# An attention layer whose query maxima and head results no longer pass TensorE's transposes

## The chip, the cores and the metric

The kernel runs on one core of a Trainium2 chip. The metric is the device time of one execution in microseconds (us); the median of several runs is given. The core has TensorE (matrix products), VectorE, ScalarE and POOL (elementwise work), and SyncE (SP), which here only issues DMA transfers.

## The reference

```python
x = L0_attn_hidden_states                          # (4, 2048, 256), fp32
xn = _layernorm(x, axis=-1)
qkv = (xn @ W_qkv).reshape(B, S, 3, NUM_HEADS, HEAD_DIM)   # 16 heads of 16
scores = jnp.einsum('bhqd,bhkd->bhqk', q, k) + compute_bias(rel_emb, S, S)
attn = jax.nn.softmax(scores, axis=-1)
out = jnp.einsum('bhqk,bhkd->bhqd', attn, v)       # -> (4, 2048, 256)
attention = out @ W_out
router_probs = softmax(xn @ router_w)              # top 2 of 8, normalised; their sum scales the FFN
ffn = (gelu(xn @ w1 + b1) @ w2 + b2) * sum(combine)
return x + attention + ffn
```

The bias depends on key position minus query position through 32 buckets; beyond 128 positions it is constant on each side. There are 4 x 16 = 64 pairs of batch and head, called heads here, each of 2048 queries and 2048 keys.

## The kernel before

It has three parts, each a block of its own.

**Part one** normalises x, makes q, k and v, and computes x + ffn into `base_rows` in DRAM. q and k are kept in DRAM (`qk_parts`) transposed, each fp32 split into a high and a low part, since TensorE multiplies the type `fp32r`; three pairs of parts stacked over 16 dimensions make the 48 rows (`ROWS`) of a product. v stays in SBUF (`v_all`). For heads 0 and 1 it also computes the row maxima (`early_scores`, 64 pairs of matmuls), since part two is two heads ahead with the maxima (`LEAD = 2`).

**Part two** is the attention, head by head, everything unrolled. A head has 16 steps `kb`, one for each block of 128 keys, and a step has four tiles `c` of 512 queries. For each tile TensorE computes the transposed scores (keys x queries) of head n into one of `RING` = 3 PSUM banks (`scores`), and beside it, on other rows of the array, one tile of query-major scores of head n + 2 into banks 3 to 6 (`maxima`), which VectorE reduces to maxima by pairs of banks. ScalarE takes the exponential of each score tile into `prob` (`PROBS` = 4 buffers of a whole step), which frees the ring bank. POOL multiplies the columns near the diagonal by the exponential of the bias (`near`). Two steps later (`LAG`) `sums` multiplies by v, whose 17th column is ones, so that bank 7 gets the weighted values and, in row 16 of each group of 32 partitions, the totals. The order on each engine is written out by hand; each waits on counted semaphores.

The maxima enter the scores as a 49th row: keys carry ones there, queries carry minus their maximum. For that `turn_shift` (L958, in step 8) transposes the maxima `max_neg` on TensorE into a ring bank, ScalarE copies them to `shift_row` (L804), and SyncE sends them to the stack (L775). The result of a head is copied out of bank 7 by ScalarE (`collect`, L810, before step 2), transposed by `turn_result` (L987, before step 4) into a ring bank, copied again (`collect_turned`, L816), and VectorE's reciprocal (L918) and POOL's `normalise` (L860) put it into the place of v. Both turns take a turn in the ring, so the ring has 66 tiles a head.

SyncE loads per head four stacks of q and k parts (L144), then the near table (L770), then the shift row.

**Part three** is the projection, for 16 chunks of 512 rows: ScalarE packs (L1097), TensorE transposes (L1158), ScalarE and VectorE make high and low parts (L1108, L1127), TensorE multiplies in three passes (L1171, 24 matmuls a chunk), VectorE adds the base rows (L1139), SyncE stores and loads.

Of the kernel before, what the change touches and what calls it, by code (L numbers as in the profile page):

```python
# [14 lines left out]
H, D = 16, 16  # L15
# [28 lines left out]
PROBS = 4  # L44
# [85 lines left out]
def transformer_layer(nc, x, w_qkv, w_out, rel_emb, router_w, w1, b1, w2, b2, hot, out):  # L130
# [4 lines left out]
    base_d = nc.dram_tensor("base_rows", [B * S, E], F32).ap()  # L135

    def load_stacks(sp, n, q_stack, k_stack, loaded):

        for which, stack, loads in ((0, q_stack, Q_LOADS), (1, k_stack, K_LOADS)):
            for row, part, parts, copies in loads:  # L140
                rows = qk_d[which, part:part + parts, bass.ds(D * n, D), :]
                if copies > 1:
                    rows = rows.to_broadcast([copies, D, S])
                sp.dma_start(stack[D * row:D * (row + parts * copies), :].bitcast(F32), rows).then_inc(loaded, 16)  # L144

    ctx = ExitStack()
    with ctx:
# [21 lines left out]
        with c1:  # L169
# [419 lines left out]
            def _(pe):  # L589
# [22 lines left out]
                def early_scores(b, c, piece):  # L612
# [3 lines left out]
                    for h in range(2):  # L616
                        last = nc.tensor.matmul(ps[:, h], q_early[HALF * h:HALF * h + ROWS, P * i:P * (i + 1)],  # L617
                                                k_early[HALF * h:HALF * h + ROWS, CH * j:CH * (j + 1)], start=True, stop=True)
# [78 lines left out]

        c2 = ExitStack()  # L700
        with c2:
# [3 lines left out]
            ones_row = sb("ones_row", [1, S], F32R, c=c2)  # L705
# [4 lines left out]
            max_neg = sb("max_neg", [P, 2, KB], c=c2)  # L710
            shift_row = sb("shift_row", [KB, 2, P], F32R, c=c2)
            o_sb = sb("o_sb", [P, CH], c=c2)
            o_turned_sb = sb("o_turned_sb", [P, TPC, CPB, 32], c=c2)
            recip = sb("recip", [P, TPC, CPB], c=c2)
# [6 lines left out]
            v_ones_set = sem("v_ones_set")  # L721
            score_ready = sem("score_ready")
# [6 lines left out]
            shift_turned = sem("shift_turned")  # L729
            o_copied = sem("o_copied")  # L730
            o_turned = sem("o_turned")
            recip_done = sem("recip_done")
            o_done = sem("o_done")

            RING = 3
            MAX_BANK = RING
            SUM_BANK = 7


            TURN_RESULT, TURN_SHIFT = 4, 8  # L740
            RESULT_AT = CPB * TURN_RESULT
            SHIFT_AT = CPB * TURN_SHIFT + 1
            RING_TILES = CPB * KB + 2

            def tile_at(kb, c):

                return CPB * kb + c + (kb >= TURN_RESULT) + (kb >= TURN_SHIFT)

            def drained_at(n, at):


                count = RING_TILES * n + at + 1
                if isinstance(n, int):
                    count += (n == 0 and at < RESULT_AT) - (n == NH - 1 and at >= SHIFT_AT)
                return count
# [8 lines left out]
            def _(sp):  # L764
                def load(n, u):
# [4 lines left out]
                    sp.dma_start(near[u][:], near_d[bass.ds(n % H, 1)].rearrange("a p s c -> (a p) s c")).then_inc(near_in[u], 16)  # L770

                def shift(n, u):

                    wait(sp, drained, 1 if isinstance(n, int) and n == 0 else drained_at(n - 1, SHIFT_AT))
                    sp.dma_start(q_st[u][ROWS:ROWS + 1, :].bitcast(F32).rearrange("a (i p) -> a i p", p=P),  # L775
                                 shift_row[:, n % 2 if isinstance(n, int) else u % 2, :].bitcast(F32)) \
                        .then_inc(shift_in[u], 16)

                def group(g, last=False):
                    for u in range(GROUP):  # L780
                        n = GROUP * g + u
                        if not (last and u > 0):
                            load(n + GROUP - 1, (u + GROUP - 1) % GROUP)
                        if not (last and u == GROUP - 1):
                            shift(n + 1, (u + 1) % GROUP)

                load(0, 0)
                sp.wait_ge(ones_set, 1)
                for u in range(GROUP):
                    sp.dma_start(k_st[u][ROWS:ROWS + 1, :].bitcast(F32), ones_row[:].bitcast(F32)).then_inc(ones_in, 16)  # L790
                shift(0, 0)
                for u in range(1, GROUP - 1):
                    load(u, u)
                group(0)
                for g in range(1, GROUPS - 1):
                    group(g)
                group(GROUPS - 1, last=True)

            @block.scalar
            def _(act):  # L800
                def shift(n, par):

                    wait(act, shift_turned, n + 1)
                    nc.scalar.activation(shift_row[:, par % 2, :], ps[0:KB, SHIFT_AT % RING, 0:P], ACT.Copy).then_inc(drained, 1)  # L804

                def collect(n):

                    wait(act, pv_done, CPB * KB * (n + 1))
                    wait(act, o_turned, n)
                    nc.scalar.activation(o_sb[:], ps[:, SUM_BANK], ACT.Copy).then_inc(o_copied, 1)  # L810

                def collect_turned(n):

                    wait(act, o_turned, n + 1)
                    wait(act, o_done, n)
                    nc.scalar.activation(o_turned_sb[:].rearrange("p i c w -> p (i c w)"), ps[:, RESULT_AT % RING], ACT.Copy) \  # L816
                        .then_inc(drained, 1)

                def head(n, u, first=False, last=False):
                    for kb in range(KB):  # L820
                        if kb == LAG and not first:
                            collect(n - 1)
                        if kb == TURN_RESULT and not first:
                            collect_turned(n - 1)
                        if kb == TURN_SHIFT and not last:
                            shift(n + 1, (u + 1) % GROUP)
                        for c in range(CPB):
                            i = CPB * (KB * n + kb) + c
                            wait(act, score_ready, i + 1)

                            wait(act, pv_done, summed(n, kb - PROBS, c) if kb >= PROBS else summed(n - 1, KB + kb - PROBS, c))
                            nc.scalar.activation(prob[:, kb % PROBS, CH * c:CH * (c + 1)], ps[:, tile_at(kb, c) % RING], ACT.Exp).then_inc(drained, 1)  # L832

                shift(0, 0)
                for u in range(GROUP):
                    head(u, u, first=u == 0)
                for g in range(1, GROUPS - 1):
                    for u in range(GROUP):
                        head(GROUP * g + u, u)
                for u in range(GROUP):  # L840
                    head(NH - GROUP + u, u, last=u == GROUP - 1)
                collect(NH - 1)
                collect_turned(NH - 1)

            @block.gpsimd
            def _(pool):
                def build(n, u, turn):
                    wait(pool, pv_done, CPB * KB * (n - 1))
                    pool.wait_ge(v_ones_set, 2)
                    nc.gpsimd.tensor_copy(vx[:, u % 2, :, 0:D], v_all[:, bass.ds(n, 1)].rearrange("p a k d -> p (a k) d")) \  # L850
                        .then_inc(v_read, 1)

                    pool.wait_ge(near_in[u], 16 * turn)
                    wait(pool, v_read, n + 1)
                    nc.gpsimd.tensor_tensor(vr[:, u % 2], vx[:, u % 2],
                                            near[u][:, 0, 0:1].unsqueeze(2).to_broadcast([P, KB, 32]), ALU.mult).then_inc(v_built, 1)

                def normalise(n):

                    nc.gpsimd.tensor_tensor(  # L860
                        v_all[:, bass.ds(n, 1)].rearrange("p a (c i) d -> p i (a c) d", c=CPB), o_turned_sb[:, :, :, 0:D],
                        recip[:].unsqueeze(3).to_broadcast([P, TPC, CPB, D]), ALU.mult).then_inc(o_done, 1)

                def head(g, u, first=False, last=False):
                    n = GROUP * g + u
                    for kb in range(KB):
                        if kb == TURN_RESULT + 2 and not first:

                            wait(pool, recip_done, n)
                            wait(pool, v_read, n)  # L870
                        if kb == 8 and not last:
                            build(n + 1, (u + 1) % GROUP, g + 1 if u + 1 < GROUP else g + 2)
# [5 lines left out]
                        if kb == TURN_RESULT + 2 and not first:  # L878
                            normalise(n - 1)
# [329 lines left out]
```

## Time and profile before

| | us |
|---|---|
| median of 3 runs | 3470.35 |
| lowest, highest | 3449.76, 3496.86 |
| the profiled execution | 3448.83 |
| its span | 3447.1 |
| TensorE busy | 3245.1 (94%) |
| VectorE busy | 2769.0 (80%) |
| ScalarE busy | 2476.0 (72%) |
| POOL busy | 1203.8 (35%) |

The span goes from the first to the last instruction. Part one takes about the first 590 us, part three the last 70. A busy TensorE is not one at its peak, since ends of matmuls are modelled. In the rows below L numbers are lines of the kernel, PE is TensorE, PEld its weight loads, DVE VectorE, ACT ScalarE, SPq the transfers that SyncE issues.

### The profile page before, as it was taken

The numbers are of one execution on the slowest core, as the hardware profiler recorded it, in microseconds if no ns is written. First come the engines' busy times: TensorE is split into PE (matmuls) and PEld (weight loads), VectorE is DVE, ScalarE is ACT, GpSimd is POOL, SyncE is SP. The second block draws the span as 40 slices with busy tenths as digits, with TensorE's granted clock in tenths as the row PEclk, the third lists the DMA queues.
The fourth block names the chain that finished last, engine by engine and source line by source line (L and its number), as shares of the span: only waits on it lengthen the run. The fifth ranks groups of instructions, "written<-read, shape, count | busy, mean of one in ns | idle before, by whom it ended". The sixth has DMA issues, their size and how long they took to land. (4 is left out here: it accounts for less than half of the span.)

```text
span 3447.1 us, 56397 instructions
## 1 busy us (share of the span) xinstructions
PE 3245.1 (94%) x20426; PEld 1573.3 (46%) x20426; DVE 2769.0 (80%) x3046; ACT 2476.0 (72%) x4875; POOL 1203.8 (35%) x1644
## 2 busy tenths in 40 slices
PE   8899997699999999999999999999999999999998
PEld 7788886233333333333333333333333333333337
DVE  5477764588888888888888888888888888888815
ACT  4343443588878887888878888788878887888875
POOL 1112121233433344434444344333443334333430
PEclk9999999799999999999999999999999999999999
DMA  7332323100000000000000000000000000000006
GB/s 183 115 88 74 102 82 101 47 28 28 28 28 28 28 28 28 28 28 28 28 28 28 28 28 28 28 28 28 28 28 28 28 28 28 28 28 28 15 1 199
DMA packets 80480, 156.52 MB, mean 45 GB/s; under 512 B 8088, under 2 KB 48728, under 8 KB 73864
## 3 DMA queue, kind: packets, MB, share of 16 engines
q1 hardware_dynamic: 80200, 152.90, 15.5%
q8 instruction: 161, 2.64, 0.3%
q14 instruction: 119, 0.97, 0.1%
HBM read 101.92 MB, written 56.16 MB: 46 GB/s over the span
## 5 line engine op out<-in xcount | busy, mean ns | idle before, releaser
L905 DVE TENSOR_REDUCE max_half<-ps 128x1 f32<-128x1024 f32 x1984 | 2337.2, 1220 | 337.0 <-PE ps L946 333.6
L832 ACT ACTIVATE prob<-ps 128x512 f32<-128x512 f32 x4096 | 2114.8, 603 | 506.9 <-PE ps L962 506.8
L962 PE MATMUL ps<-q_st,k_st 49*128 49x512 f32 x4096 | 1511.3, 446 | 160.7 <-ACT prob L832 52.5
L946 PE MATMUL ps<-k_st,q_st 48*128 48x512 f32 x3968 | 1569.4, 468 | 0.2 <-DVE max_half L905 0.2
L876 POOL TENSOR_TENSOR prob<-prob,near 128x224 f32<-128x224 f32 (+2 forms) x1408 | 965.1, 691 | 1667.8 <-ACT prob L832 1649.0
L962 PEld LDWEIGHTS ps<-q_st,k_st 49*128 49x128 f32 x4096 | 679.2, 184 | 1334.7 <-ACT prob L832 1142.2
L971 PE MATMUL ps<-prob,vx 128*32 128x512 f32 x4096 | 947.8, 606 | 0.0
L971 PE MATMUL ps<-prob,vr 128*32 128x512 f32 x4096 | 946.1, 604 | 0.0
L946 PEld LDWEIGHTS ps<-k_st,q_st 48*128 48x128 f32 x3968 | 656.3, 184 | 58.7 <-DVE max_half L905 2.5
L608 PE MATMUL ps<-xnt,w_parts 128*128 128x512 f32 x1152 | 276.7, 400 | 16.7 <-DMA k_early<-qk_parts 10.5
L608 PEld LDWEIGHTS ps<-xnt,w_parts 128*128 128x128 f32 x1152 | 218.1, 191 | 70.1 <-DMA k_early<-qk_parts 10.7
L549 ACT ACTIVATE parts<-ps 128x512 fp32r<-128x512 f32 x64 | 38.1, 598 | 272.0 <-PE ps L608 232.6
L971 PEld LDWEIGHTS ps<-prob,vr 128*32 128x32 f32 x4096 | 133.1, 108 | 172.9 <-ACT prob L832 144.9
L673 PE MATMUL ps<-w_parts,hid 128*128 128x256 f32 x1536 | 196.7, 284 | 0.0
L673 PEld LDWEIGHTS ps<-w_parts,hid 128*128 128x128 f32 x1536 | 184.2, 189 | 11.7 <-issue 11.7
L971 PEld LDWEIGHTS ps<-prob,vx 128*32 128x32 f32 x4096 | 132.5, 108 | 78.7 <-ACT prob L832 53.2
L360 POOL TENSOR_TENSOR top_exp<-euler,top_less 128x32 f32<-128x32 f32 x16 | 86.8, 5428 | 160.7 <-DVE top_less L413 160.7
L354 POOL TENSOR_TENSOR rstd<-var_eps,power 128x4 f32<-128x4 f32 x17 | 23.1, 1359 | 307.6 <-DVE var_eps L388 307.6
L557 ACT ACTIVATE hid_raw<-ps,b_sb 128x512 f32<-128x512 f32 x128 | 88.2, 690 | 42.3 <-PE ps L608 32.6
L458 DVE TENSOR_TENSOR parts<-ps,parts 128x512 fp32r<-128x512 f32 x64 | 44.1, 692 | 71.6 <-ACT parts L549 71.6
L475 DVE TENSOR_TENSOR hid<-hid_raw,hid 128x512 fp32r<-128x512 f32 x128 | 85.4, 688 | 19.3 <-ACT hid L564 17.9
L448 DVE TENSOR_REDUCE max_early<-ps 128x2 f32<-128x1024 f32 x64 | 78.4, 1225 | 19.2 <-PE ps L617 18.9
(70 smaller groups left out, 1060.4 us busy)
## 6 DMA issues: line engine op xcount, KB each, us to landing
qk_parts<-parts SPq DMA_DIRECT2D x64, 512.0 KB, 4.6
near<-bias_near SPq DMA_DIRECT2D x64, 352.0 KB, 13.4
q_st<-qk_parts SPq DMA_DIRECT2D x64, 256.0 KB
k_st<-qk_parts SPq DMA_DIRECT2D x64, 256.0 KB
x_sb<-in_L_attn_hidden_states SPq DMA_DIRECT2D x18, 512.0 KB, 6.1
base_rows<-x_sb SPq DMA_DIRECT2D x16, 512.0 KB, 2.9
q_st<-qk_parts SPq DMA_DIRECT2D x64, 128.0 KB
k_st<-qk_parts SPq DMA_DIRECT2D x64, 128.0 KB
```

The lines of the kernel that those rows point to most:

```text
L360: nc.gpsimd.tensor_tensor(top_exp[:], euler[:], top_less[:], ALU.pow).then_inc(exp_done, 1)
L448: nc.vector.tensor_reduce(max_early[:, :, bass.ds(i, 1), j], ps[:, 0:2].unsqueeze(2), AX.X, ALU.max).then_inc(max_done, 1)
L475: nc.vector.tensor_tensor(hid[:, 1, f], hid_raw[:, f % RAWS], hid[:, 0, f].bitcast(F32), ALU.subtract).then_inc(hid_low, 1)
L557: nc.scalar.activation(hid_raw[:, f % RAWS], ps[:, F1_BANKS[f % 4]], ACT.Gelu_apprx_tanh, bias=b1_sb[:, f:f + 1]) \
L608: last = nc.tensor.matmul(to, stationary(a, k), moving(b, k), start=k == 0 and (a, b) == PASSES[0], stop=k == blocks - 1 and (a, b) == PAS ...
L673: last = nc.tensor.matmul(ps[:, F2_BANKS[t % 2], E * (t // 2):E * (t // 2 + 1)], hid[:, a, f, P * t:P * (t + 1)], weight(W_2, b_, f), star ...
L832: nc.scalar.activation(prob[:, kb % PROBS, CH * c:CH * (c + 1)], ps[:, tile_at(kb, c) % RING], ACT.Exp).then_inc(drained, 1)
L876: nc.gpsimd.tensor_tensor(prob[:, kb % PROBS, q0:q1], prob[:, kb % PROBS, q0:q1], near[u][:, side, c0:c0 + q1 - q0], ALU.mult).then_inc(ne ...
L905: nc.vector.reduce_max(max_half[:, par % 2, i, half:half + 1], ps[:, MAX_BANK + 2 * half:MAX_BANK + 2 + 2 * half].rearrange("p a n -> p (a ...
L946: mm = nc.tensor.matmul(ps[:, MAX_BANK + c], q_st[u][0:ROWS, P * i:P * (i + 1)], k_st[u][0:ROWS, CH * c:CH * (c + 1)], start=True, stop=True)
L962: nc.tensor.matmul(ps[:, tile_at(kb, c) % RING], k_st[u][:, P * kb:P * (kb + 1)], q_st[u][:, CH * c:CH * (c + 1)], start=True, stop=True). ...
L971: nc.tensor.matmul(ps[32 * c:32 * (c + 1), SUM_BANK], v[:, u % 2, kb], prob[:, kb % PROBS, CH * c:CH * (c + 1)], start=kb == 0, stop=kb == ...
```

## The change

The query blocks of the maxima are strided: block i holds queries i, 16 + i, 32 + i and so on. Then `max_neg`, partition p and column i, is minus the maximum of query 16 p + i, and it goes to the query row by one transfer as it lies. Results stay transposed: the four total rows of `o_sb` are sent to 128 partitions of 16 (`totals`), VectorE takes reciprocals, SyncE stores them to DRAM and spreads each to 16 partitions (`spread`), POOL multiplies (`normalise`), and SyncE keeps the rows in the order of the projection's operand (`keep`), for batches 1 to 3 in the place of v of the batch before. The projection follows in the same block: no pack, no turn, the low part made by POOL, the output weight and the first base rows loaded during head 1. `PROBS` is 3, the ring has 64 tiles a head, `o_sb` is double.

```diff
-PROBS = 4
+PROBS = 3
+    def query_block(stack, i):
+        return stack.rearrange("r (p i) -> r i p", i=KB)[:, i]
@@ early scores and maxima (TensorE)
-  q_early[HALF * h:HALF * h + ROWS, P * i:P * (i + 1)]
+  query_block(q_early[HALF * h:HALF * h + ROWS], i)
-  q_st[u][0:ROWS, P * i:P * (i + 1)]
+  query_block(q_st[u][0:ROWS], i)
@@ sync
-                def shift(n, u):
-                    wait(sp, drained, 1 if isinstance(n, int) and n == 0 else drained_at(n - 1, SHIFT_AT))
-                    sp.dma_start(q_st[u][ROWS:ROWS + 1, :].bitcast(F32).rearrange("a (i p) -> a i p", p=P),
-                                 shift_row[:, n % 2 if isinstance(n, int) else u % 2, :].bitcast(F32)) \
+                def shift(n):
+                    wait(sp, neg_done, n + 1)
+                    sp.dma_start(q_st[n % GROUP][ROWS:ROWS + 1, :].bitcast(F32).rearrange("a (p i) -> a p i", i=KB),
+                                 max_neg[:, n % 2].bitcast(F32)).then_inc(shift_in[n % GROUP], 16)
+                def totals(n):
+                    sp.wait_ge(o_copied, n + 1)
+                    wait(sp, recip_done, n)
+                    for c in range(CPB):
+                        sp.dma_start(total_sb[32 * c:32 * (c + 1)], o_sb[32 * c + D:32 * c + D + 1, n % 2].rearrange("a (g i) -> a g i", i=PIECE)) \
+                            .then_inc(total_in, 16)
+                def spread(n):
+                    sp.wait_ge(recip_done, n + 1)
+                    sp.dma_start(recip_d[n].rearrange("(p i) -> p i", i=PIECE), recip[:]).then_inc(recip_stored, 16)
+                    sp.wait_ge(recip_stored, 16 * (n + 1))
+                    wait(sp, o_done, n)
+                    for c in range(CPB):
+                        sp.dma_start(recip_rows[32 * c:32 * c + D], recip_d[n:n + 1, CH * c:CH * (c + 1)].to_broadcast([D, CH])).then_inc(recip_in, 16)
+                def keep(n):
+                    sp.wait_ge(o_done, n + 1)
+                    for c in range(CPB):
+                        sp.dma_start(attn[b][D * (h % (P // D)):D * (h % (P // D) + 1), h // (P // D), CH * c:CH * (c + 1)],
+                                     o_sb[32 * c:32 * c + D, n % 2]).then_inc(attn_in[b], 16)
+                for n in range(NH):
+                    if n + GROUP - 1 < NH:
+                        load(n + GROUP - 1)
+                    if n + 1 < NH:
+                        shift(n + 1)
+                    if n > 0:
+                        totals(n - 1)
+                        spread(n - 1)
+                        keep(n - 1)
+                    if n == 1:
+                        sp.dma_start(wo_raw[:], w_out.rearrange("(k p) n -> p k n", p=P)).then_inc(wo_in, 16)
+                        for c in range(CPB):
+                            load_base(0, c)
@@ scalar: collect_turned and shift are gone
+                high(0)
+                high(1)
+                collect(NH - 1)
+                for i in range(2, B * CPB):
+                    high(i)
@@ gpsimd, TOTAL_AT, NORM_AT = 6, 10
+                def normalise(n):
+                    pool.wait_ge(recip_in, 16 * CPB * (n + 1))
+                    nc.gpsimd.tensor_tensor(o_sb[:, n % 2], o_sb[:, n % 2], recip_rows[:], ALU.mult).then_inc(o_done, 1)
+                def low(i):
+                    pool.wait_ge(a_high, i + 1)
+                    nc.gpsimd.tensor_tensor(turned[:, i % 2, 1], attn[b][:, :, CH * c:CH * (c + 1)], turned[:, i % 2, 0].bitcast(F32),
+                                            ALU.subtract).then_inc(a_low, 1)
@@ vector, after the maxima of step TOTAL_AT
+                def reciprocals(n):
+                    dve.wait_ge(total_in, 16 * CPB * (n + 1))
+                    wait(dve, recip_stored, 16 * n)
+                    nc.vector.reciprocal(recip[:], total_sb[:]).then_inc(recip_done, 1)
@@ tensor: ring_free, turn_shift, turn_result and part three's turn are gone
```

TensorE, a stretch inside a head around the result turn, before (L962 are scores, L946 maxima, L971 sums, L987 the turn):

```order
L962 MATMUL ps<-q_st,k_st 128x512
L946 MATMUL ps<-k_st,q_st 128x512
L971 MATMUL ps<-prob,vx 32x512 x4
L987 MATMUL ps<-ident,o_sb 128x128 x4
L962 MATMUL ps<-q_st,k_st 128x512
L946 MATMUL ps<-k_st,q_st 128x512
```

and after (L1014 scores, L1005 maxima, L1029 sums):

```order
L1014 MATMUL ps<-q_st,k_st 128x512
L1005 MATMUL ps<-k_st,q_st 128x512
L1029 MATMUL ps<-prob,vx 32x512 x4
L1014 MATMUL ps<-q_st,k_st 128x512
L1005 MATMUL ps<-k_st,q_st 128x512
L1014 MATMUL ps<-q_st,k_st 128x512
```

The sums are followed by the next step's first score at once, in every step.

SyncE, one head, before (stacks, near table, shift row):

```order
L770 DMA near<-bias_near 128x704
L775 DMA q_st<-shift_row 1x16x128
L144 DMA q_st<-qk_parts 32x1x2048
L144 DMA q_st<-qk_parts 16x2048
L144 DMA k_st<-qk_parts 32x1x2048
L144 DMA k_st<-qk_parts 16x2048
```

and after:

```order
L145 DMA k_st<-qk_parts 16x2048
L783 DMA near<-bias_near 128x704
L788 DMA q_st<-max_neg 1x128x16
L796 DMA total_sb<-o_sb 32x1x16 x4
L802 DMA recip_all<-recip 128x16
L808 DMA recip_rows<-recip_all 16x512 x4
L817 DMA attn_first<-o_sb 16x512 x4
L145 DMA q_st<-qk_parts 32x1x2048
```

Thirteen transfers are added between a head's shift row and the next head's stacks, in three groups with a wait each.

POOL, the end of the program after the change (L927 the near multiplies, L935 the low parts, L917 the last head's normalisation); before, the near multiplies and one normalisation ended it:

```order
L927 TENSOR_TENSOR prob<-prob,near 128x352 x2
L927 TENSOR_TENSOR prob<-prob,near 128x224
L935 TENSOR_TENSOR turned<-attn_first,turned 128x1024 x2
L917 TENSOR_TENSOR o_sb<-o_sb,recip_rows 128x512
L935 TENSOR_TENSOR turned<-attn_first,turned 128x1024 x2
L935 TENSOR_TENSOR turned<-v_all,turned 128x1024 x12
```

The low parts of chunks 2 to 15 stand behind the normalisation of the last head.

## Rows read from the trace of the kernel before

**Rows 1.** Windows: us, then busy us by engine (instructions), clock, DMA share, GB/s.

```profile
680.00:3350.00 2670.00, 2555.16 (x16186) 1006.37 (x16186) 2317.13 (x2073) 2139.30 (x4180) 1062.30 (x1559) 1.00 0.09 27
```

**Rows 2.** Timeline of ScalarE in one head: start, us, instruction, idle before it.

```profile
1453.54 2.06 ACT L832 ACTIVATE prob<-ps 128x512 f32<-128x512 f32 x4 [0.54 <-PE ps L962]
1456.31 0.60 ACT L816 ACTIVATE o_turned_sb<-ps 128x512 f32<-128x512 f32 x1 [0.70 <-PE ps L987]
1456.80 2.06 ACT L832 ACTIVATE prob<-ps 128x512 f32<-128x512 f32 x4
1459.41 2.07 ACT L832 ACTIVATE prob<-ps 128x512 f32<-128x512 f32 x4 [0.55 <-PE ps L962]
...
1464.64 2.07 ACT L832 ACTIVATE prob<-ps 128x512 f32<-128x512 f32 x4 [0.55 <-PE ps L962]
...
1467.46 2.06 ACT L832 ACTIVATE prob<-ps 128x512 f32<-128x512 f32 x4 [0.16 <-PE ps L962]
```

**Rows 3.** Timeline of TensorE's weight loads in one plain step.

```profile
1504.30 0.18 PEld L962 LDWEIGHTS ps<-q_st,k_st 49*128 49x128 f32 x1 [0.84 <-ACT prob L832]
...
1505.49 0.18 PEld L962 LDWEIGHTS ps<-q_st,k_st 49*128 49x128 f32 x1 [0.40 <-ACT prob L832]
...
1505.49 0.18 PEld L946 LDWEIGHTS ps<-k_st,q_st 48*128 48x128 f32 x1
...
1505.92 0.11 PEld L971 LDWEIGHTS ps<-prob,vx 128*32 128x32 f32 x2 [0.25 <-ACT prob L832]
```

**Rows 4.** Timeline of VectorE, two steps.

```profile
1502.49 2.36 DVE L905 TENSOR_REDUCE max_half<-ps 128x1 f32<-128x1024 f32 x2 [0.15 <-PE ps L946]
1505.11 2.36 DVE L905 TENSOR_REDUCE max_half<-ps 128x1 f32<-128x1024 f32 x2 [0.26 <-PE ps L946]
```

**Rows 5.** Timeline of weight loads in the last head, without maxima.

```profile
3359.62 0.18 PEld L962 LDWEIGHTS ps<-q_st,k_st 49*128 49x128 f32 x1 [0.66 <-ACT prob L832]
...
3360.04 0.11 PEld L971 LDWEIGHTS ps<-prob,vr 128*32 128x32 f32 x2 [0.24 <-issue]
```

**Rows 6.** Groups by shape: count, busy us, mean ns of one, idle before.

```profile
L946 PEld LDWEIGHTS ps<-k_st,q_st 48*128 48x128 f32 x3968 | 656.3, 184 | 58.7 <-DVE max_half L905 2.5
L876 POOL TENSOR_TENSOR prob<-prob,near 128x352 f32<-128x352 f32 x512 | 481.7, 941 | 940.6 <-ACT prob L832 940.6
L876 POOL TENSOR_TENSOR prob<-prob,near 128x96 f32<-128x96 f32 x384 | 150.5, 392 | 265.6 <-ACT prob L832 265.6
L971 PEld LDWEIGHTS ps<-prob,vr 128*32 128x32 f32 x4096 | 133.1, 108 | 172.9 <-ACT prob L832 144.9 <-issue 28.1
L918 DVE RECIPROCAL recip<-o_turned_sb 128x16 f32<-128x16 f32 x64 | 15.7, 245 | 89.2 <-ACT o_turned_sb L816 89.2
L421 DVE RECIPROCAL total<-total 128x4 f32<-128x4 f32 x16 | 2.9, 178 | 0.6
```

**Rows 7.** Transfers in 1400 to 1600 (KB, median us to landing), and SyncE's issues.

```profile
near<-bias_near SPq DMA_DIRECT2D x5, 352.0 KB, 14.0
...
q_st<-shift_row SPq DMA_DIRECT2D x5, 8.0 KB, 1.8
...
1446.33 0.42 SPq L770 DMA_DIRECT2D near<-bias_near  x1
1467.33 0.56 SPq L775 DMA_DIRECT2D q_st<-shift_row  x1
```

**Rows 8.** The last part: timelines of three engines, and a window of 10 us.

```profile
3369.37 2.06 ACT L832 ACTIVATE prob<-ps 128x512 f32<-128x512 f32 x4 [0.54 <-PE ps L962]
...
3388.57 3.11 PE L1171 MATMUL ps<-wo_parts,turned 128*128 128x256 f32 x24
...
3388.42 0.38 SPq L1074 DMA_DIRECT2D out_rows<-base_in  x1
...
3437.04 6.99 SPq L1074 DMA_DIRECT2D out_rows<-base_in  x3
...
3420.00:3430.00 10.00, 10.00 (x88) 10.00 (x87) 7.38 (x18) 5.70 (x17) 0.00 (x0) 1.00 0.93 279
```

More of the change, by code:

```diff
@@ L779, in group @@
[L779 to L787, printed above, removed]
+                    sp.dma_start(near[u][:], near_d[n % H:n % H + 1].rearrange("a p s c -> (a p) s c")).then_inc(near_in[u], 16)
@@ L788, in _ @@
+                load(0)
                 sp.wait_ge(ones_set, 1)
                 for u in range(GROUP):
[L790 to L826, printed above, removed]
-                        for c in range(CPB):
[L828 to L843, printed above, removed]
@@ new lines, in head @@
+                def head(n):
+                    for kb in range(KB):
+                        if kb == LAG and n > 0:
+                            collect(n - 1)
+                        for c in range(CPB):
+                            act.wait_ge(score_ready, tile_at(n, kb, c) + 1)
+                            t = KB * n + kb
+                            if t >= PROBS:
+                                act.wait_ge(pv_done, summed((t - PROBS) // KB, (t - PROBS) % KB, c))
+                            nc.scalar.activation(prob[:, t % PROBS, CH * c:CH * (c + 1)], ps[:, tile_at(n, kb, c) % RING], ACT.Exp) \
+                                .then_inc(drained, 1)
@@ new lines, in high @@
+                def high(i):
+                    b, c = i // CPB, i % CPB
+                    act.wait_ge(attn_in[b], 16 * CPB * H)
+                    wait(act, proj_ready, TPC * (i - 1))
+                    nc.scalar.activation(turned[:, i % 2, 0], attn[b][:, :, CH * c:CH * (c + 1)], ACT.Copy).then_inc(a_high, 1)
+                for n in range(NH):
+                    head(n)
+                    if n == 2:
+                        act.wait_ge(wo_in, 16)
+                        nc.scalar.activation(wo_parts[:, 0], wo_raw[:], ACT.Copy).then_inc(wo_high, 1)
@@ new lines, in _ @@
+                for m in range(LEAD):
+                    combine(m, max_early)
+                for n in range(NH):
+                    for kb in range(KB):
+                        if n + LEAD < NH:
+                            maxima(n + LEAD, kb)
+                        if kb == TOTAL_AT and n > 0:
+                            reciprocals(n - 1)
+                    if n + LEAD < NH:
+                        combine(n + LEAD, max_half)
+                    if n == 3:
+                        dve.wait_ge(wo_high, 1)
+                        nc.vector.tensor_tensor(wo_parts[:, 1], wo_raw[:], wo_parts[:, 0].bitcast(F32), ALU.subtract).then_inc(wo_low, 1)
@@ L1150, in _ @@
+                reciprocals(NH - 1)
+                for i in range(B * CPB):
+                    b, c = i // CPB, i % CPB
+                    for t in range(TPC):
+                        dve.wait_ge(proj_ready, TPC * i + t + 1)
+                        if t == 0:
+                            dve.wait_ge(rows_in[c], 16 * (b + 1))
+                        nc.vector.tensor_tensor(base_in[:, c, t], base_in[:, c, t], ps[:, PROJ_BANK + t, 0:E], ALU.add).then_inc(res_done, 1)
             @block.tensor
@@ new lines, in _ @@
+                for n in range(NH):
+                    m = n + LEAD
+                    for kb in range(KB):
+                        if kb == 0:
+                            pe.wait_ge(shift_in[n % GROUP], 16 * (n // GROUP + 1))
+                            if n < GROUP:
+                                pe.wait_ge(ones_in, 16 * GROUP)
+                                pe.wait_ge(stacks_in[n], 16 * STACK_LOADS)
+                            if m < NH:
+                                pe.wait_ge(stacks_in[m % GROUP], 16 * STACK_LOADS * (m // GROUP + 1))
+                        for c in range(CPB):
+                            scores(n, kb, c)
+                            if m < NH:
+                                maxima(m, kb, c)
+                        t = KB * n + kb - LAG
+                        if t >= 0:
+                            sums(t // KB, t % KB)
@@ L1156, in turn @@
+                for kb in range(KB - LAG, KB):
+                    sums(NH - 1, kb)
+                pe.wait_ge(wo_low, 1)
+                pe.wait_ge(max_done, 2 * KB * NH)
+                for i in range(B * CPB):
+                    pe.wait_ge(a_low, i + 1)
                     for t in range(TPC):
+                        wait(pe, res_done, TPC * (i - 1) + t + 1)
                         for k in range(KE):
-                            last = nc.tensor.transpose(ps[:, TURN_BANKS[c % 2] + k, P * t:P * (t + 1)], rows[:, c % 2, t, P * k:P * (k + 1)],
-                                                       ident[:])
@@ L1178, in _ @@
-                turn(0, 0)
-                turn(1, 1)
-                pe.wait_ge(wo_low, 1)
-                batch(0)
-                for b in range(1, B - 1):
-                    batch(b)
-                batch(B - 1)
+                            for x, y in PASSES:
+                                last = nc.tensor.matmul(ps[:, PROJ_BANK + t, 0:E], turned[:, i % 2, x, k, P * t:P * (t + 1)], wo_parts[:, y, k],
+                                                        start=k == 0 and (x, y) == PASSES[0], stop=k == KE - 1 and (x, y) == PASSES[-1])
@@ L1188 @@
+                        last.then_inc(proj_ready, 1)
 _INS = ["L0_attn_hidden_states", "L0_attn_W_qkv", "L0_attn_W_out", "L0_attn_rel_emb", "L0_ffn_router_w",
```

419 lines of the change are left out of this document (134 added, 285 removed).

## The prediction

> **What bounds the kernel now.** I read the windows by stage first, then the timelines of ScalarE, TensorE and VectorE inside one head, then the groups with their mean durations, then the transfers, then the last part. In the 2670 us of attention that the first row covers [rows 1] TensorE is busy 96%, VectorE 87%, ScalarE 80%; a busy share does not say which of them sets the pace, so the step has to be read.
>
> A head is 16 steps of four tiles. ScalarE's rows [rows 2] give the clock: 1456.80 to 1459.41 is a plain step, 2.61 us, of which ScalarE works 2.06 and waits 0.55 for the next score tile. The loop that sets this is in TensorE's rows [rows 3]: the fourth score tile of a step (1505.49) waits until the first exponential has emptied one of the three ring banks; 0.43 us later (1505.92) the sums begin; they hold TensorE until the next step's first score, which started 1.19 us before the fourth (1504.30). ScalarE cannot start the next step before that score. So every extra thing TensorE does between the fourth score and the next first one lengthens the step, and nothing on VectorE does as long as it stays under 2.61: its two reductions take 2.36 and it then waits 0.26, or 0.15 in the step after a small reciprocal [rows 4]. In the last two heads, which have no maxima, fourth score to sums is 0.42 [rows 5]: today the maxima ride beside the scores for nothing.
>
> Two steps of a head are longer [rows 2]. The one with the result turn goes from 1453.54 to 1456.80, 3.26 us, 0.65 over 2.61: four transposes stand in the gap and ScalarE copies a bank. The one with the shift turn goes from 1464.64 to 1467.46, 2.82, 0.21 over.
>
> **The change, part by part.**
>
> *Turns removed.* 63 result turns lie inside heads (the 64th is at the end) and 63 shift turns do. Both their TensorE work and ScalarE's copies stood in the loop, so their excess is the gain: 63 x (0.65 + 0.21) = 54.2 us. The copy of the sums out of PSUM stays, as does its small excess. What is late next is the loop itself at 2.61 us.
>
> *Strided query blocks.* 3968 weight loads of the maxima now take every 16th fp32 of a row (64 bytes apart) in place of 128 neighbours. No row shows TensorE reading so. Where it would cost: the fourth maxima of a step is issued right beside the fourth score, both loads start together at 1505.49 [rows 3], and the sums, which use all 128 rows of the array, start when both have streamed. So the extra ns of one load per step are on the path: 62 heads with maxima x 16 = 992 steps, and the other three loads of a step have a few tenths of slack. The 64 early pairs in the first part add 64 more. One ns of extra load is 1.056 us of kernel. Bounds: below, nothing (a load can't get shorter by being strided). Above, the nearest row in which an engine walks single fp32 values far apart is VectorE's reciprocal of 16 values 128 bytes apart, 245 ns, against 178 ns for 4 neighbours [rows 6]: 5.6 ns per value, the slow operation itself included. A contiguous weight load costs (184 - 108) / 96 = 0.79 ns per column [rows 6], so the far end is 128 x 4.8 = 0.61 us, +650 us. I take nothing: the load's own pace of 0.79 ns per fp32 is slower than that of the moving side (24 x 256 columns in 3.11 us [rows 8], 0.51 ns each), so the read has some room, and the reciprocal's price is mostly an operation that no load does. I hold this value loosely; it carries the first rival.
>
> *Fewer probability buffers, 4 to 3.* The exponential of step k waits for the sums of step k-3. TensorE issues those before the scores of step k, and the exponential needs such a score anyway. Nothing; the cover is TensorE's own order.
>
> *Maxima straight to the query row.* One transfer of 128 short pieces in place of 16 longer ones; the old one landed in 1.8 us [rows 7], and it has a whole head (42 us). Nothing, even at 15 us.
>
> *The way of the sums.* Per head SyncE issues 13 more transfers (4 sums, 1 store, 4 spreads, 4 keeps) at 0.4 to 0.6 us [rows 7]: about 7 us of 42. They stand behind the stacks and the near table, whose transfer is issued at 1446.33 and lands 14.0 us later [rows 7], at 1460.3. The sums are copied between steps 1 and 2, so they leave soon after 1450.9 (a step before 1453.54), and may land only about 1460.5 to 1461. VectorE asks for them after step 6: step 3 begins at 1453.54, step 6 then at 1461.4, its reductions end at 1464.0. Margin 3 us. Then reciprocal 0.25, store 0.6 + 1.8, four spreads 2.2 + 1.8: about 1470.5. POOL asks after its multiply of step 10, whose exponentials begin at 1453.54 + 7 x 2.61 = 1471.8. Margin over 1 us, and the sums of a step run two steps behind, so one late multiply is forgiven. Nothing. Queued behind those waits are, on VectorE, the maxima of step 7 (and behind them TensorE), on SyncE only the keeps, and the next head's loads 16 us later.
>
> *POOL.* The new normalisation of 512 columns, by the near multiplies' slope (941 - 392) / 256 = 2.14 ns per column [rows 6], is 392 + 416 x 2.14 = 1.28 us. With a 0.94 multiply in that step it makes 2.2 of 2.61. Nothing.
>
> *The last part.* Before: last exponentials end at 3371.43, then the kept sums, a new block, weights, packs and turns; the first result is stored at 3388.42 and then one chunk every (3437.04 - 3388.42) / 13 = 3.74 us [rows 8]. In that stretch TensorE is always busy but the transfers are too, 0.93 of all engines at 279 GB/s [rows 8]. So taking away eight transposes a chunk can't bring 0.7 us: 0.93 x 3.74 = 3.48 is what a chunk's load and store need. POOL's low part of 1024 columns is 392 + 928 x 2.14 = 2.38 us by the same slope, ScalarE's high part at most 2 x 0.60; with two buffers and 3.1 us of projection [rows 8] that is (2.4 + 1.1 + 0.2 + 3.1) / 2 = 3.4. I take 3.5 a chunk. The start: projections 0 and 1 run at about 3375 to 3381, 8 us earlier than now; but POOL's next item is the last head's normalisation, which waits for 4 transfers (4.0), reciprocal (0.25), store (2.4), 4 transfers (4.0) after a copy at about 3374 (two steps' sums of about 1 us each, then 0.6), so 3384.6; then 1.3 and 2.4 more put projection 2 at 3388.3. Fourteen chunks x 3.5 = 49 give 3437.3, and about 4 for the last add and store 3441, against 3447.1. I take 5 us of gain, with ends of -2 and +10.
>
> The copy of the output weight moves under the attention part, 0.6 us on ScalarE once, nothing.
>
> **Sum.** 3448.8 (the profiled execution) - 54.2 - 5 = 3389.6, 1.7% faster. The three runs shown have a median of 3470.35, 21.5 above the profiled one, with the lowest at 3449.76, so that one is at the bottom of the scatter; the same ratio on the median would be 3411. I put the median of the changed kernel between, at 3400. Two per cent, which is about what a measurement of this kernel can tell from no change, is 69 us.
>
> **Rivals.**
>
> *A: strided loads cost time.* Place: the fourth maxima of each step, ahead of the sums. If each column takes twice as long, +0.79 x 128 = 101 ns, +107 us, 3496 (1.4% slower). It eats the gain from 56 ns on. From 121 ns on the kernel is over 2% slower; if the whole load doubles, +184 ns, it is 3584 (3.9% slower). For it: 64-byte steps are new to this engine here, and there is no slack at that place. Against it: the load's slow own pace. The Trainium skill, SBUF — State Buffer, section "Door 1: The DMA port swizzle", speaks for it: lines are 16 bytes, two hits in a line are needed for full bandwidth, and for fp32 a step of up to four is free; a step of 16 breaks that. No row here shows whether it binds TensorE's load; by a rule of one line per column at half pace the time would be the 3496 above, by the row-based choice 3390. Chance 0.22 for 25 to 121 ns, 0.10 above.
>
> *B: VectorE becomes the bound.* It has 2.36 busy in 2.61, and the reciprocal (0.25) and the combination (0.19) no longer fall beside a stretched step. If both went on the path: 62 x 0.44 = 27 us, 3417. Against it: before, the next reduction after a reciprocal still waited 0.15 for TensorE [rows 4]. Chance 0.08.
>
> *C: the sums come late.* If the transfers queued behind the near table land 2 us after VectorE asks, at 1466, VectorE, then TensorE, stand still in each head: 63 x 2 = 126 us, 3516 (1.9% slower). Against it the margin of 3 us. Chance 0.08.
>
> That leaves 0.52 for the forecast. The range 3375 to 3510 holds the forecast with its tail's ends and the scatter, B, most of A's middle case and half of C: about 0.82. Over 2% faster needs the forecast and a scatter in its favour, 0.22; over 2% slower is A's upper case, half of C and a little of A's middle, 0.18; within 2% 0.60.
>
> **What would show it.** The weight loads of the maxima at 184 ns, or longer, decide A, and with them fourth score to sums at 0.43 us. The step of 2.61 everywhere but where the sums are copied, and a head of about 41.95 us, show the turns' gain. VectorE rows waiting for a transfer would show C; a step above 2.61 with VectorE never idle, B. In the last part: a TensorE gap of some 7 us after the second projection, then 3.5 us a chunk. The prediction is wrong if the load got longer by more than some 20 ns.

## The result and the profile after

The changed kernel takes 3499.9 us (median of 20 runs, 3496.41 to 3545.01), the kernel before, with more runs, 3454.19 (20 runs, 3449.76 to 3496.86). The ratio is 1.0144, 95% interval [1.0107, 1.0181]: slower by 1.4%, where 1.7% faster was forecast. That is less than the two per cent the prediction calls hard to tell from no change, but the interval lies wholly above 1. The time is inside the range and 4 us from the rival called A.

Both kernels' times fall into three groups 20 to 24 us apart: of the changed kernel's 20 runs 12 take 3496.4 to 3500.4 us, two 3519 to 3520 and six 3541 to 3545, and of the kernel before's 11 take 3449.8 to 3454.7, six 3470 to 3472 and three 3494 to 3497. The profiled execution of the changed kernel, 3519.31 us with a span of 3517.5, is of the middle group, and in its trace the last head runs at half of TensorE's clock; that of the kernel before (3448.83) is of the lowest. No kept trace is of the highest group; that there both of the last two heads run at half clock is an estimate from the distance (43 to 45 us, twice the 21 of one head) and from the mean granted clock of the whole run (0.987 to 0.990 in the lowest group, 0.980 and 0.981 in the middle, 0.970 to 0.972 in the highest). The medians of the lowest groups compare as 3498.6 to 3451.4, 47 us.

ScalarE's copies of the head sums divide the spans. Timeline of ScalarE, kernel before; copies of heads 0, 62 and 63:

```profile
680.37 0.60 ACT L810 ACTIVATE o_sb<-ps 128x512 f32<-128x512 f32 x1 [0.23 <-PE ps L971]
...
3334.43 0.60 ACT L810 ACTIVATE o_sb<-ps 128x512 f32<-128x512 f32 x1 [0.22 <-PE ps L971]
3373.37 0.60 ACT L810 ACTIVATE o_sb<-ps 128x512 f32<-128x512 f32 x1 [1.94 <-PE ps L971]
```

and the changed kernel:

```profile
691.36 0.60 ACT L868 ACTIVATE o_sb<-ps 128x512 f32<-128x512 f32 x1 [0.33 <-PE ps L1029]
...
3392.72 0.60 ACT L868 ACTIVATE o_sb<-ps 128x512 f32<-128x512 f32 x1 [0.22 <-PE ps L1029]
3452.58 0.60 ACT L868 ACTIVATE o_sb<-ps 128x512 f32<-128x512 f32 x1 [2.77 <-PE ps L1029]
```

Up to the first copy 11.0 us are lost: the last block of part one starts 7.3 later (571.55 to 578.81), TensorE's wait between the parts is 1.4 longer, and head 0 takes 2.3 more. Over 62 heads 2654.1 becomes 2701.4 (+47.3). The last head goes from 38.9 to 59.9 (+20.9, the half clock), and from the last copy to the end 73.7 becomes 64.9 (-8.8). Together +70.4, the difference of the spans.

Something that neither kernel addresses shows in the same stretch. In both, TensorE stands nearly idle for some 48 to 49 us between part one and the first score (before from 583.1 to 631.1, after from 590.4 to 639.8), waiting at its end for the first stacks of k, and then works at a granted clock of 0.50 for about 11 us (before) and 13 us (after). That is nearly as much as the turns are worth.

Inside a head, ScalarE's timeline after, around the place where the result turn was:

```profile
1476.23 0.60 ACT L868 ACTIVATE o_sb<-ps 128x512 f32<-128x512 f32 x1 [0.33 <-PE ps L1029]
...
1479.43 2.06 ACT L880 ACTIVATE prob<-ps 128x512 f32<-128x512 f32 x4 [0.65 <-PE ps L1014]
1482.15 2.07 ACT L880 ACTIVATE prob<-ps 128x512 f32<-128x512 f32 x4 [0.66 <-PE ps L1014]
```

The steps of 3.26 and 2.82 of [rows 2] are gone, and every plain step is 2.71 to 2.72 instead of 2.61. Why, is in the weight loads of one step (start, us; L1014 scores, L1005 maxima, L1029 sums), which answer [rows 3]:

```profile
1500.63 0.18 PEld L1014 LDWEIGHTS ps<-q_st,k_st 49*128 49x128 f32 x1 [0.84 <-ACT prob L880]
...
1501.82 0.18 PEld L1014 LDWEIGHTS ps<-q_st,k_st 49*128 49x128 f32 x1 [0.32 <-ACT prob L880]
...
1501.82 0.29 PEld L1005 LDWEIGHTS ps<-k_st,q_st 48*128 48x128 f32 x1
...
1502.35 0.11 PEld L1029 LDWEIGHTS ps<-prob,vr 128*32 128x32 f32 x2 [0.25 <-ACT prob L880]
...
1503.35 0.18 PEld L1014 LDWEIGHTS ps<-q_st,k_st 49*128 49x128 f32 x1 [0.84 <-ACT prob L880]
```

First to fourth score is 1.19 us as before; fourth score to sums is 0.53, where it was 0.43; sums to next first score is 1.00. The fourth maxima's load lasts 0.29 beside a score's 0.18; that the sums wait for it is shown by the pair of runs on the four loads, below. The groups answer [rows 6]:

```profile
L1005 PEld LDWEIGHTS ps<-k_st,q_st 48*128 48x128 f32 x3968 | 1085.1, 297 | 49.0 <-DVE max_half L960 2.6
...
L917 POOL TENSOR_TENSOR o_sb<-o_sb,recip_rows 128x512 f32<-128x512 f32 x64 | 82.3, 1286 | 8.0 <-DMA recip_rows<-recip_all 8.0
L935 POOL TENSOR_TENSOR turned<-v_all,turned 128x1024 fp32r<-128x1024 f32 x12 | 28.8, 2396 | 14.2 <-ACT turned L888 14.2
```

VectorE's timeline around a reciprocal shows that it is neither the bound nor waiting for a transfer; compare [rows 4]:

```profile
1487.93 2.35 DVE L960 TENSOR_REDUCE max_half<-ps 128x1 f32<-128x1024 f32 x2 [0.36 <-PE ps L1005]
1490.20 0.25 DVE L974 RECIPROCAL recip<-total_sb 128x16 f32<-128x16 f32 x1
1490.65 2.36 DVE L960 TENSOR_REDUCE max_half<-ps 128x1 f32<-128x1024 f32 x2 [0.20 <-PE ps L1005]
```

Last, windows of the last two heads, first in the changed kernel (us, then busy us of TensorE, weight loads, VectorE, ScalarE, POOL; granted clock; DMA share; GB/s). Between the two windows, at about 3394, the clock falls from 1.00 to 0.50, that is from 2.4 to 1.2 GHz, although both heads do the same work (scores and sums, no maxima):

```profile
3352.00:3392.00 40.00, 36.59 (x189) 12.63 (x189) 0.25 (x1) 31.97 (x64) 17.69 (x25) 1.00 0.03 8
3395.00:3445.00 50.00, 50.00 (x152) 15.74 (x144) 0.25 (x1) 25.20 (x49) 13.00 (x19) 0.50 0.03 6
```

and in the kernel before, at the start of head 62:

```profile
3290.00:3330.00 40.00, 36.85 (x180) 12.90 (x176) 0.25 (x1) 30.79 (x61) 15.43 (x23) 0.96 0.00 1
```

There the clock dipped for a few us and came back. Head 62 took 44.10 us between the copies where the heads ahead of it took 42.8, so this trace of the lowest group holds 1.3 us of it.

### The profile page after: what moved, and what is told of

Same layout as the page of the kernel before. It is cut to its first block, busy times and chain, and to the rows that moved or that the text cites. A ratio compares the mean times of both kernels' runs of the same rounds, so it can differ in the third digit from the quotient of the medians.

```text
span 3517.5 us, 55995 instructions
## 1 busy us (share of the span) xinstructions
PE 3402.6 (97%) x19978; PEld 1823.5 (52%) x19978; DVE 2752.3 (78%) x3014; ACT 2407.5 (68%) x4667; POOL 1284.1 (37%) x1661
## 4 chain that ended last, share of the span: by engine, by line
PE 77%; ACT 3%; issue 1%; DMA 1%; SPq 1%; POOL 1%; DVE 0%; ACTq 0%
PE ps L1014 32%; PE ps L1029 30%; PE ps L1005 14%; ACT prob L880 2%; DMA k_st<-qk_parts 1%; PE ps L1062 1%; POOL turned L935 0%; SPq L145 0%; ACT turned L888 0%; SPq L829 0%; ACT o_sb L868 0%; DMA recip_rows<-recip_all 0%; DMA total_sb<-o_sb 0%; SPq L796 0%; DMA recip_all<-recip 0%
## 5 line engine op out<-in xcount | busy, mean ns | idle before, releaser
L1005 PE MATMUL ps<-k_st,q_st 48*128 48x512 f32 x3968 | 1761.0, 524 | 0.2 <-DVE max_half L960 0.2
L927 POOL TENSOR_TENSOR prob<-prob,near 128x224 f32<-128x224 f32 (+2 forms) x1408 | 964.6, 691 | 1694.3 <-ACT prob L880 1675.6
L1014 PE MATMUL ps<-q_st,k_st 49*128 49x512 f32 x4096 | 1506.0, 448 | 74.3 <-DMA k_st<-qk_parts 49.4
L1014 PEld LDWEIGHTS ps<-q_st,k_st 49*128 49x128 f32 x4096 | 685.2, 186 | 1268.3 <-ACT prob L880 1140.3
L1005 PEld LDWEIGHTS ps<-k_st,q_st 48*128 48x128 f32 x3968 | 1085.1, 297 | 49.0 <-DVE max_half L960 2.6
L1029 PE MATMUL ps<-prob,vx 128*32 128x512 f32 x4096 | 960.0, 613 | 0.0
L1029 PE MATMUL ps<-prob,vr 128*32 128x512 f32 x4096 | 958.1, 612 | 0.0
L1029 PEld LDWEIGHTS ps<-prob,vr 128*32 128x32 f32 x4096 | 133.9, 108 | 174.4 <-ACT prob L880 169.5
L1029 PEld LDWEIGHTS ps<-prob,vx 128*32 128x32 f32 x4096 | 133.1, 108 | 79.3 <-ACT prob L880 62.5
L974 DVE RECIPROCAL recip<-total_sb 128x16 f32<-128x16 f32 x64 | 15.6, 244 | 110.0 <-DMA total_sb<-o_sb 110.0
```

Of the source, the lines that this page charges most:

```text
L927: nc.gpsimd.tensor_tensor(at, at, near[n % GROUP][:, side, c0:c0 + q1 - q0], ALU.mult).then_inc(near_done, 1)
L1005: mm = nc.tensor.matmul(ps[:, MAX_BANK + c], query_block(q_st[u][0:ROWS], i), k_st[u][0:ROWS, CH * c:CH * (c + 1)], start=True, stop=True)
L1014: nc.tensor.matmul(ps[:, at % RING], k_st[u][:, P * kb:P * (kb + 1)], q_st[u][:, CH * c:CH * (c + 1)], start=True, stop=True).then_inc(sco ...
L1029: nc.tensor.matmul(ps[32 * c:32 * (c + 1), SUM_BANK], v[:, n % 2, kb], prob[:, (KB * n + kb) % PROBS, CH * c:CH * (c + 1)], start=kb == 0, ...
```

## The experiments

Each kernel is compared with the kernel before on the same chip. Because of the groups of times, the lowest run is given with the median: with four runs, a median can lie between two groups.

**Neighbouring blocks in the changed kernel.**

```diff
-        return stack.rearrange("r (p i) -> r i p", i=KB)[:, i]
+        return stack[:, P * i:P * (i + 1)]
```

> The changed kernel, but a maxima block is again 128 neighbouring queries; the one transfer of the maxima is left as it is, so that each query is shifted by the maximum of another one (this alters the computation's scaling only, not its instructions). Theory (the strided weight loads are the whole loss): loads of the maxima back from 297 to 184 ns, plain step from 2.715 to 2.61 us, part one 7 us shorter; 992 x 0.105 + 7 = 111 us less than the changed kernel's 3499.9, so about 3387, a head about 41.95 us. Rival (the new transfers, POOL's longer work or three probability buffers lengthen the step): the step stays above 2.65 us and the time stays near 3480.

Measured: 3387.95 us median, 3387.02, 3387.32, 3388.58 and 3431.0; ratio to before 0.9832 [0.975, 0.9914]. Its loads and ScalarE's timeline:

```profile
L1005 PEld LDWEIGHTS ps<-k_st,q_st 48*128 48x128 f32 x3968 | 657.0, 184 | 72.3 <-DVE max_half L960 3.0
```

```profile
1499.96 2.07 ACT L880 ACTIVATE prob<-ps 128x512 f32<-128x512 f32 x4 [0.55 <-PE ps L1014]
1502.57 2.07 ACT L880 ACTIVATE prob<-ps 128x512 f32<-128x512 f32 x4 [0.54 <-PE ps L1014]
```

The step is 2.61 again and a head takes 41.92 us (forecast 41.95), with all thirteen transfers, POOL's longer work and three buffers in place. The lowest group is 111 us under the changed kernel's (3387 to 3498.6), so the strides are the whole loss, and the rest of the change gains 62 us (3450 to 3387).

**The strides alone, in the kernel before.**

```diff
-  mm = nc.tensor.matmul(ps[:, MAX_BANK + c], q_st[u][0:ROWS, P * i:P * (i + 1)], ...
+  mm = nc.tensor.matmul(ps[:, MAX_BANK + c], q_st[u][0:ROWS].rearrange("r (p i) -> r i p", i=KB)[:, i], ...
```

> The kernel before with one edit: the maxima blocks of part two are strided by 16 (each query is then shifted by another one's maximum, which only rescales). Theory: the loads take 297 ns, the step 2.61 -> 2.715, so 3454 + 992 x 0.105 = 3558 (3.0% slower), turns in place, a head about 44.4 us. Rival (the load's length is hidden when the rest of the change is absent): unchanged at 3454.

Measured: 3550.16 us median (3550.07 to 3571.73), ratio 1.0292 [1.0211, 1.0372]; loads 297 ns, plain steps 2.71 to 2.72. That is 100 us above the median of the kernel before beside it (3449.8), 0.101 for each of 992 steps, a little under the 0.105 forecast. The cost needs nothing else of the change.

**Every 2nd query, and every 4th.** `STEP` is 2 or 4:

```diff
+SHIFTS = S // P // STEP
-        return stack.rearrange("r (p i) -> r i p", i=KB)[:, i]
+        return stack.rearrange("r (g p j) -> r g j p", j=STEP, p=P)[:, i // STEP, i % STEP]
+                    for g in range(SHIFTS):
+                        sp.dma_start(q_st[n % GROUP][ROWS:ROWS + 1, P * STEP * g:P * STEP * (g + 1)].bitcast(F32).rearrange("a (p j) -> a p j", j=STEP),
+                                     max_neg[:, n % 2, STEP * g:STEP * (g + 1)].bitcast(F32)).then_inc(shift_in[n % GROUP], 16)
```

> The changed kernel with blocks that take every 2nd query (8 bytes apart) of 256, and the maxima sent by 8 transfers of 8-byte pieces. Theory with 16-byte lines of which two hits are needed: 2 values in a line, loads at 184 ns, time about 3390. Rival (any step costs): loads at 240 to 297 ns, time 3445 to 3500. Second rival (4 KB of 8-byte pieces are too slow for the query row): TensorE waits for a transfer at each head's start.

> As the last, but every 4th query (16 bytes apart) of 512, the maxima in 4 transfers of 16-byte pieces. Each value is in a new 16-byte line. Theory (a new line for each value costs the full price): loads at 297 ns, time about 3500. Rival (a step of up to four fp32 is free, as the skill's page on SBUF also says): loads at 184 ns, time about 3390.

Measured for a step of 2: 3390.92 us median, all four runs within 3389.64 to 3391.99, ratio 0.981 [0.9751, 0.9869]. For a step of 4: 3514.42, 3515.77, 3558.82 and 3559.2, median 3537.29, ratio 1.0233 [1.0142, 1.0323]. The group of the maxima's loads with step 2, then with step 4:

```profile
L1008 PEld LDWEIGHTS ps<-k_st,q_st 48*128 48x128 f32 x3968 | 687.6, 192 | 69.6 <-DVE max_half L963 3.7
```

```profile
L1008 PEld LDWEIGHTS ps<-k_st,q_st 48*128 48x128 f32 x3968 | 1138.5, 311 | 35.7 <-DVE max_half L963 2.6
```

8 bytes apart costs 8 ns, 16 bytes apart 127 and 64 bytes apart 113. The edge lies between 8 and 16 bytes; a step of three was not run. The Trainium skill (SBUF — State Buffer, "Door 1: The DMA port swizzle") has two statements on this: at least two hits in a line of 16 bytes for full bandwidth, and strides of up to four fp32 for free. The first fits these runs (two values in 16 bytes 192 ns, one 297 or 311), the second does not: a step of four took 311 ns. Why 16 bytes cost 14 ns more than 64 stays open. The version with a step of 2 beats both kernels and keeps each query's own maximum. Its 8 small transfers a head (8 KB together, not the 4 KB of the expectation) cost little: the step is 2.61, a head takes 41.88 to 42.39 us where with neighbouring blocks it takes 41.87 to 42.04, and the whole takes 3 us more than neighbouring blocks do (3390.9 to 3388.0).

**Which of the four loads is on the path.** In part one and where not named, blocks are neighbours:

```diff
-  query_block(q_st[u][0:ROWS], i)
+  query_block(q_st[u][0:ROWS], i) if c < 3 else q_st[u][0:ROWS, P * i:P * (i + 1)]     # first three
+  query_block(q_st[u][0:ROWS], i) if c == 3 else q_st[u][0:ROWS, P * i:P * (i + 1)]    # fourth
```

> The changed kernel with neighbouring blocks in part one and for the fourth maxima tile of a step, strided by 16 for the first three (the maxima then mix queries, which alters only the scaling). Theory on the place (only the load beside the fourth score is on the path): three of four loads at 297 ns, yet the step is 2.61 to 2.63 us and the time 3388 to 3400. Rival (the loads share one budget and any of them delays the step): three quarters of the loss stays, step 2.69, time about 3466.

> The reverse of the last: only the fourth tile's load is strided. Theory: the whole loss of part two is back, step 2.715, 3388 + 992 x 0.105 = 3492. Rival: a quarter of it, 3414.

As in the first two experiments, queries are then shifted by each other's maxima, which serves to measure and is not a version to keep. Measured: three strided loads in a step 3388.38 us median (3386.60, 3387.48, 3389.27, 3409.08), the fourth alone 3512.48 (3490.24, 3491.84, 3533.13, 3536.5), ratios 0.9794 [0.9723, 0.9864] and 1.014 [1.0055, 1.0224]. Lowest against lowest, three quarters of the longer loads cost nothing, and one quarter costs all: 3490.24 - 3386.60 = 103.6 us, 0.104 for each of 992 steps. The loads, first three and then fourth:

```profile
L1005 PEld LDWEIGHTS ps<-k_st,q_st 48*128 48x128 f32 x3968 | 979.5, 269 | 142.5 <-DVE max_half L960 69.8
```

```profile
L1005 PEld LDWEIGHTS ps<-k_st,q_st 48*128 48x128 f32 x3968 | 761.5, 211 | 2.5 <-DVE max_half L960 2.5
```

With three, the step is 2.61 at a mean load of 269 ns, and fourth score to sums is 0.42; with the fourth alone it is 2.71 at 211 ns, and 0.54. Mean load time and loss go opposite ways.

**A filler for the last two heads.** Added to the step-2 version, to the changed kernel and to the kernel before:

```diff
                             if m < NH:
                                 maxima(m, kb, c)
+                            else:
+                                filler(m, kb, c)     # the same matmul on old stacks into banks 3 to 6, unread
```

> The kernel with blocks of every 2nd query, and in the last two heads, which have no maxima to compute, TensorE issues the same maxima matmuls on old stacks into the four free banks, unread. Theory (TensorE's clock falls to half in these heads in some executions since it does less there, which gives the groups of times 21 and 44 us above the lowest): every run lies within 4 us of 3391, and no stretch of the last two heads shows a granted clock of 0.5; the fillers ride beside the scores, so a last head costs 0.2 us more at most. Rival (the fall comes from something outside the kernel): one run in three is still 20 or 44 us above the lowest.

> The changed kernel with unread maxima matmuls (neighbouring blocks) in the last two heads. Theory (the half clock comes from the thinner work of these heads): all six executions within 5 us of the lowest group, 3497 to 3501, granted clock 1.00 through both heads. Rival (it comes from elsewhere): about 8 in 20 executions of the changed kernel lay 20 or 44 us above, so two of six would here.

> The same filler in the kernel before. Theory: all six executions within 5 us of 3451. Rival: one or two of six at 3471 or 3493, as the kernel before beside it shows.

Measured, step 2 with filler: 3390.61, 3390.74, 3391.51, 3392.08, 3394.16 and one of 8949.91, for which nothing in the kernel accounts and which stays unexplained; median 3391.8. The changed kernel with filler: 3496.25 to 3497.34 in all four runs, median 3496.59. The kernel before with filler: 3447.47 to 3453.1 in all eleven, median 3450.41; the kernel before beside it had 13 of 15 within 3447.5 to 3452.33, and 3492.98 and 3493.99. A window across the last two heads of the changed kernel with filler:

```profile
3375.00:3415.00 40.00, 36.57 (x248) 12.59 (x248) 0.25 (x1) 32.16 (x64) 14.48 (x22) 1.00 0.03 8
```

Twenty of twenty runs with filler, the odd one aside, are in the lowest group. How often a kernel without filler is above it differs between sets of runs (17 of 40 in the first, 2 of 15 in the last), so the fair comparison is with what ran beside them: on the same two chips 8 of 34 runs without filler were above (5 of 26 of the kernel before, 3 of 8 of the pair on the four loads). If the filler did nothing, all eight would fall among the runs without it with a chance of under 2%. Each version alone shows less: the step-2 version had none above in four runs without filler either, and a window at clock 1.00, like the one shown, is found in the lowest group without filler too. So it is shown in a trace that a last head at half clock makes the middle group, and made likely, not proved, that the unread matmuls keep the clock up. Whether it matters that they run on the idle rows of the array, or only that there are more of them, was not tested.

## Why the prediction was wrong

**The failed step is the price of a strided weight load.** It was taken as 0, "held loosely"; it is 113 ns. The step argued from the load's own pace (0.79 ns per column against the moving side's 0.51) that the read has room, and the runs show no room at a step of 16: 297 ns for 184. The rest of that step was right in the main. The place is only the load beside the fourth score, shown by the pair of runs on that, and the count is 992 steps. The price passes on to the step a little less than whole: over heads 1 to 61 (976 steps, between ScalarE's copies) the changed kernel takes 102.6 us more than the version with neighbouring blocks, 0.105 a step for 113 ns of load, and the version with a step of 4 takes 117.4 more, 0.120 for 127. In part one 128 loads went from 183 to 288 ns. Its last block starts at 570.6 to 573.1 us in six traces with neighbouring early blocks and at 578.8 and 579.9 in two with a step of 16, 7.6 later in the mean, where 64 x 0.113 = 7.2. By the prediction's own sum, 1.056 x 113 = 119 us on 3390 is 3509; the lowest group has 3498.6. Of the 10 us between, the smaller price per step is about 8 and the last part about 4, with about 1 us the other way left over.

**Why the row misled.** A load at 0.79 ns per column was read as slack against the moving side's 0.51. With strides it is (297 - 184) / 128 = 0.88 ns more per column, about as much again. So a slow pace with neighbours was no sign of a margin; what inside the load sets either pace no run shows. The rival that was worked out from a doubled pace, 3496, had the price within 12 ns.

**The turns** were right. In the version with neighbouring blocks, 62 heads take 2598.8 us between the copies of the sums (684.7 to 3283.5) against 2654.1, 55.3 less, where 54.2 was the sum for 63. Of this 1.3 us is the dip of the clock in head 62 of the kernel before; without it the gain is 54.0, against 62 x 0.86 = 53.3.

**Nothing from the three buffers, the new transfers, POOL and VectorE** was right. The totals landed 2.7 us after their issue, earlier than thought, and VectorE waited for them only behind its last maxima, where it has nothing else to do. POOL's prices by the slope of the near multiplies came out at 1.286 us for 1.28 and 2.396 for 2.38.

**The last part** gained 8.8 us for a forecast of 5, inside its ends of -2 and +10. The mechanism holds: after the second projection TensorE waits for POOL, which waits 8 us for the last head's reciprocals, and then two chunks take 6.8 us, 3.4 each where 3.5 was taken. The sign given for it, a gap of some 7 us, came out at 3.55 in this trace. The second projection ended late here, since it waited 1.94 us for VectorE and ran 4.23. In the trace of the changed kernel with filler, with no half clock ahead of it, it ran 3.11 and the gap is 4.67. The way of the last sums was also shorter than forecast: from the end of their copy (3453.18) to POOL's start (3461.60) 8.4 us, where 10.65 was added up. That puts about 2 of the extra 4 us there; the faster chunks give 1.4. TensorE's timeline after, to be read against [rows 8]:

```profile
3457.44 4.23 PE L1062 MATMUL ps<-wo_parts,turned 128*128 128x256 f32 x24 [1.94 <-DVE base_in L996]
3465.22 7.50 PE L1062 MATMUL ps<-wo_parts,turned 128*128 128x256 f32 x48 [3.55 <-POOL turned L935]
3473.53 6.01 PE L1062 MATMUL ps<-wo_parts,turned 128*128 128x256 f32 x48 [0.81 <-POOL turned L935]
3480.33 6.04 PE L1062 MATMUL ps<-wo_parts,turned 128*128 128x256 f32 x48 [0.79 <-POOL turned L935]
```

**The scatter** was seen (21.5 us between profile and median) and not asked about. The three first times of the kernel before, 3450, 3470 and 3497, were one of each group. The prediction put its median at 3400, between two groups, where no run of a version near the forecast lay: those of the version with neighbouring blocks were 3387 to 3389 and 3431.

## What to carry to other kernels

Removing a transpose by striding TensorE's stationary operand trades one short operation per head for a longer load in every step; with a step of 2 (8 bytes) a load of 128 columns costs 8 ns more and the trade is nearly free, with a step of 4 or 16 it costs 127 or 113. Before costing a longer load, find the one that the next operation waits for: three of four here were free. If a kernel's runs fall into groups, compare the granted clock stretch by stretch, above all where an engine's work thins out, before taking the spread for noise.

## What the runs showed of the hardware

- Loads of 128 fp32 columns on 48 rows took 184 ns with neighbours, 192 at 8 bytes, 311 at 16 and 297 at 64.
- A load longer by 113 or 127 ns ahead of matmuls on all rows lengthened the step by 105 or 120; three such loads elsewhere in the step cost 0.001 us a step.
- Without the maxima, a stretch of scores and sums (36.6 busy us of 40) ran at a granted clock of 1.00 in one head and at 0.50 in the next (profile of the changed kernel), and at 1.00 in both in other traces. A head with half clock cost about 21 us here (steps of 4.07 instead of 2.60). With unread matmuls beside the scores 20 of 20 runs were in the lowest group, against 26 of 34 without on the same chips, and they cost nothing measurable (ratio 0.9984 [0.9953, 1.0014]).
- After some 48 us with TensorE nearly idle, its granted clock was 0.50 for about the first 11 us of work (before) and 13 us (after).
